# Eight PSUM banks of a pre-norm transformer layer shared out anew: four for scores and three for the ring, in place of three and four

## The reference

```
h   = ln(x);  q, k, v = h @ Wq + bq, h @ Wk + bk, h @ Wv + bv        (per head: 2048 x 16)
s   = q k^T / 4 + slope[head] * (key - 2047);  s = -inf where key > query
y   = x + (softmax(s) v) @ Wo + bo
W'  = clip(round(W / (mean|W| + 1e-8)), -1, 1)    for w1, w2 (704 x 256) and w3 (256 x 704)
g   = ln(y);  out = y + (sigmoid(g W1'^T) * (g W2'^T)) W3'^T
```

## Time and profile before

| | us |
|---|---|
| median of 3 runs | 667.93 |
| the runs | 667.62 to 674.13 |
| the profiled execution's own time | 665.75 |
| its span | 664.0 |

### The profile page before, as it was taken

How to read it: one execution, slowest core, us unless ns; L and a number is a source line. 1 busy time by engine, 2 the same in 40 slices (tenths; PEclk the granted TensorE clock), 3 DMA queues, 4 the chain that set the end, 5 groups by cost and what they waited for, 6 DMA issues and landing times.

```text
span 664.0 us, 11006 instructions
## 1 busy us (share of the span) xinstructions
PE 616.9 (93%) x3710; PEld 378.2 (57%) x3710; DVE 461.9 (70%) x1189; ACT 365.4 (55%) x770; POOL 117.2 (18%) x146
## 2 busy tenths in 40 slices
PE   1888898899999989999999999999999999999997
PEld 1444555556576656455556676555555556665586
DVE  4458878667777876568787778788788888411075
ACT  2424454564464555657656556476676665667521
POOL 5465200031021220420002122003100000123000
PEclk9959898899999999999999999999999999999999
DMA  8664554465121313633231131137141210011000
GB/s 254 173 185 132 147 148 114 114 195 147 34 81 35 97 34 98 182 110 94 54 82 34 34 98 33 49 103 172 39 113 34 68 50 0 2 43 42 1 17 32
DMA packets 27277, 57.65 MB, mean 87 GB/s; under 512 B 5397, under 2 KB 15125, under 8 KB 23637
## 3 DMA queue, kind: packets, MB, share of 16 engines
q1 hardware_dynamic: 27220, 56.95, 31.6%
HBM read 41.87 MB, written 14.80 MB: 85 GB/s over the span
## 4 chain that ended last, share of the span: by engine, by line
PE 76%; DVE 11%; issue 4%; ACT 4%; DMA 3%; SPq 1%; POOL 0%; ACTq 0%; POOLq 0%
PE pS L942 19%; PE pO L955 19%; PE pM L922 17%; PE pM L897 5%; DVE pm L1094 4%; PE pM L843 3%; PE pM L906 3%; DVE pM L1097 3%; PE pS L945 2%; PE pM L883 2%; DMA qst<-mT 2%; ACT probs L787 1%; PE pS L906 1%; PE pS L843 1%; PE pM L849 1%
## 5 line engine op out<-in xcount | busy, mean ns | idle before, releaser
L787 ACT ACTIVATE probs<-pS 128x512 f32<-128x512 f32 (+3 forms) x640 | 304.8, 545 | 191.6 <-PE pS L945 94.8
L1094 DVE TENSOR_REDUCE pm<-pM 128x1 f32<-128x512 f32 x384 | 239.2, 680 | 49.4 <-PE pM L922 49.2
L942 PE MATMUL pS<-qst,kst 128*128 128x512 f32 (+3 forms) x640 | 250.4, 407 | 7.8 <-DMA qst<-mT 4.3
L922 PE MATMUL pM<-kst,qst 126*128 126x512 f32 (+3 forms) x640 | 239.4, 402 | 9.8 <-DVE pm L1097 3.4
L942 PEld LDWEIGHTS pS<-qst,kst 128*128 128x128 f32 x640 | 121.5, 192 | 91.1 <-issue 52.8
L1097 DVE CUSTOM_DVE_ANT_0 pM<-pM,mask 128x128 f32<-128x128 f32 (+3 forms) x256 | 118.5, 518 | 47.3 <-PE pM L922 47.0
L922 PEld LDWEIGHTS pM<-kst,qst 126*128 126x128 f32 x640 | 122.8, 197 | 36.6 <-DVE pm L1097 7.7
L955 PE MATMUL pO<-probs,vals 128*17 128x512 f32 (+3 forms) x1280 | 133.5, 535 | 0.0
L955 PEld LDWEIGHTS pO<-probs,vals 128*17 128x17 f32 x1280 | 29.5, 97 | 64.6 <-issue 41.0
L945 PE MATMUL pS<-maskb,identb 128*128 128x128 bf16 x256 | 58.6, 231 | 0.0
L644 POOL TENSOR_TENSOR rstd<-ve,mhalf 128x4 f32<-128x4 f32 (+1 forms) x9 | 8.5, 946 | 218.9 <-DVE ve L1010 218.8
(11 more groups left out here) (145 smaller groups left out, 426.2 us busy)
## 6 DMA issues: line engine op xcount, KB each, us to landing
kst<-parts SPq DMA_DIRECT2D x80, 256.0 KB
parts<-qk_hl SPq DMA_DIRECT2D x32, 256.0 KB, 3.2
qst<-parts SPq DMA_DIRECT2D x32, 256.0 KB, 4.1
ctx_dram<-ctx_raw SPq DMA_DIRECT2D x15, 256.0 KB, 3.9
xin<-in_L_attn_x SPq DMA_DIRECT2D x5, 512.0 KB, 5.1
out<-work SPq DMA_DIRECT2D x8, 256.0 KB, 2.2
work<-ctx_dram SPq DMA_DIRECT2D x7, 256.0 KB
work<-rden_dram SPq DMA_DIRECT2D x7, 256.0 KB
```

The source lines that it names most:

```text
L787: nc.scalar.activation(probs[:, n % PSLOTS, q0:CH], pS[:, n % SBANKS, q0:CH], ACT.Exp)\
L922: pe.matmul(max_bank(x)[:, 0:N], qst[0:R_MAX, u % QSLOTS, h, t * P:(t + 1) * P], kst[0:R_MAX, n % KSLOTS, h, 0:N], start=True, stop=True). ...
L942: ins = pe.matmul(pS[:, n % SBANKS, q0:CH], kst[0:R_END, sl, h, b:b + P], qst[0:R_END, u % QSLOTS, h, q0:CH], start=True, stop=not is_diag ...
L1094: nc.vector.tensor_reduce(dst, bank, AX.X, ALU.max).then_inc(max_free, 1)
```

## The change

One line: the score banks become four and the ring three. pO keeps its bank. With it change: the bank of every score (n % 4), what it waits for (the exponential four before), the bank of each use of the ring and what it waits for (the use three before), and the places of the head's and the tail's groups (i % 5). In the head the groups numbered 0, 5 and 10 (xT of chunk 0, the second query group of chunk 0, gamma) take the ring, where before 0, 4, 8 and 12 did. The plan of turns and side groups is the same.

```diff
-    SBANKS, RING, SIDE_AFTER = 3, 4, 1
+    SBANKS, RING, SIDE_AFTER = 4, 3, 1
```

## The result

The changed kernel takes 703.09 us (median of 4 runs, 701.78 to 706.54); the kernel before, run beside it on the same chip, takes 671.03 (667.62 to 674.16). The ratio is 1.0487, with a 95% interval of 1.0407 to 1.0567: slower by 4.9%. The forecast was slower, 685.0 with a range of 675 to 698. The direction is right, the size is 18 us short, and the range does not hold it. The profiled executions say the same: 703.06 against 665.75, spans 701.3 against 664.0. So +37.3 us where +17.5 was forecast. By the medians it is +32.1: the profiled execution of the kernel before, 665.75, lies under all four of this set, and 3.1 of the 18 us come from the kernel before itself, 671.03 in this set where the forecast started from 667.93.

A forecast was written before the change was run, and what follows sets the result against it. TensorE's order of issue was taken to bound the kernel; ring 24, score banks -8 and head 1.5 gave +17.5 us on 665.75, 683.3, or 685 with the median 2.2 higher; range 675 to 698.

The forecast's parts named there:

- What bounds the kernel: Plain pairs of steps: TensorE's order of issue sets the time, 5.78 us a pair; VectorE is next, 0.9 us to spare.
- Part 1: Ring of three, nine plain pairs: the last turn before the batch starts 0.29 us late, pair 6.07 us instead of 5.78.
- Part 2: Ring of three, fuller pairs: at most one 0.60 us slot lost per stretch between batches; ring total 24 us, ends 18 and 43.
- Part 3: Four score banks: a fourth bank removes nearly all score waits on exponentials; 8 us gained, ends 4 and 10.
- Under 10 us: Sign at the scores' weight loads: waits of L942 on L787 fall from 26.6 us to under 10.
- Part 4: Head and tail on five places: first score about 2.1 us later, costing 1.5 (ends 0 and 2.1); tail 0.
- A: Rival, faster: score banks bind and VectorE's idle time hides the ring's lateness; only -10 left, 658 us; chance 0.03.
- B: Rival, no change: TensorE headroom absorbs full slots, only plain and half of middle pairs pay; 666 to 668 us; chance 0.07.
- D: Rival, the clock: at 0.95 from 156 to 577 us, 22 us more; with the forecast +40, 707 us; chance 0.02.
- C: Rival, much slower: side groups hold one of three ring banks, every stretch pays a slot; +36, 704 us; chance 0.10.
- the pair of rows 5: Sign: the fuller pair from 547.07 us, whose ninth turn waits for the sixth reduction instead of the fifth, takes 0.6 us more.
- The waits of L922: Sign at the turns' weight loads: their waits on VectorE (L1094 and L1097) grow from 14.5 us to some 35.

The follow-up runs named there:

- e1: Changed kernel with three score banks instead of four, ring of three kept, one bank of PSUM unused: 706.18 us, ratio 1.0596 to the kernel before.
- e2b: Against the kernel before: three score banks, ring of three for turns and swaps only, side groups in their own bank; second run, for its trace: 686.51 us, ratio 1.0282.
- e12: Kernel before with the side group behind the third head instead of the second: 681.53 us, ratio 1.0165.
- e13: Changed kernel with the side group behind the third head instead of the second: 711.37 us, ratio 1.0624 to the kernel before.
- e10: Against the kernel before: three score banks, ring of three for turns only, side groups in their own bank, weighted sums every step: 678.89 us, ratio 1.0143.
- e3: Changed kernel with the head's groups back on four places instead of five: 699.93 us, ratio 1.0509 to the kernel before.
- e11: Changed kernel with the head's and the tail's groups back on their four old places: 700.07 us, ratio 1.0462 to the kernel before.
- e4: Changed kernel with a batch of weighted sums every step instead of every second step: 697.21 us, ratio 1.0457 to the kernel before.
- e5: Kernel before with a batch of weighted sums every step instead of every second step: 668.33 us, ratio 0.9997.
- e9: Kernel before with a batch per step in 33 pairs chosen from e5's timeline, double batches elsewhere: 670.79 us, ratio 1.0036.

## Why the prediction was right or wrong

**What bounds the kernel: right.** TensorE's order of issue sets the time, and one bank fewer makes a user that already waits one slot later: the first up group and the plain pairs show it in the timeline of the changed kernel, and e1 puts the whole loss on the ring.

**Part 1: place and wait right, size 0.12 short.** The last turn of a plain pair is 0.29 us late; the pair takes 6.19 us, not 6.07. The term left out is that a matmul which waits for its bank waits with its weight load, which otherwise runs under the matmul before it. Over nine pairs that is about 1 us.

**Part 2: the step that failed.** It said that the slot is lost "once per stretch between batches and not once per turn, since the waits before it in a stretch are replaced, not added". With no side group in the stretch that holds on the average: the five pairs with over 8 turns lose 0.60 us each in e1, from 0.13 to 0.96. With one, it does not. TensorE makes no turn for 1.06 us and more, and the group holds one of the three banks for 2.10 us, until its reader comes. In the stretch from 241.30 VectorE is dry in front of the group's result and the turn behind it waits for the group's bank; that stretch loses two slots, +1.21 us. Reckoned again by Part 2's own rule from the trace of the kernel before, with the largest lateness of a stretch capped at a slot, some 18 us of its sum fall on the 37 pairs with a side group; they lose 26.5 in e1, more than the 22.2 of one slot each, and 23 of the 37 lose more than a slot. With the group in a bank of its own (e2b) the 37 lose 8.1. So that the sharing costs 16 to 21 us is shown. How it does so is shown for single stretches only: that each dry place of VectorE costs one slot is not, since e12 and e13 speak against it. The cause is not settled to the last microsecond either: e10 leaves 10 us that neither the sharing nor the long batch explains.

A second gap in Part 2: "the rest nothing (few turns, or none)". The seven pairs with 1 to 6 turns lose 4.2 us in e1: 0.5 in each of three pairs with five turns in late units (4.76 to 5.24 us in one), and 1.1 in a pair with six. No run shows why. All pairs together lose 39.0 us to the ring where Part 2 took 24 with an upper end of 43. The upper end was near, with a slot for every stretch; that is a sum that fits, since the single pairs come out anywhere from 2.1 us shorter to 2.9 longer.

**Part 3: at its lower end or in the range, not settled.** Forecast 8 us, ends 4 and 10. The spans of e1 and the changed kernel differ by 3.0, but in these also lie the head's places and a tail that ended 1.5 us later. By the sums of pairs the fourth score bank gives 4.6 us in the changed kernel, 5.4 in e3 and 3.2 in e11. By the medians, each over its own kernel before, it gives 7.4, 6.3 and 8.5; e1 and e3 were timed on one chip in one set, 706.18 against 699.93. The expected gain is there in the pairs without turns, 3.8 us, within the 2 to 4 given for them. In all pairs with turns together the traces of the three kernels have between 1.7 us gained and 0.5 lost. There a score that comes earlier mostly makes the turn behind it wait longer, as the forecast said of the full stretches alone. The estimate also counted waits that are none. The first weight load behind a batch shows 0.85 us of idle time in every kernel here (0.64, 0.42 or 0.21 behind batches that end with a block on the diagonal, whose rows are narrower), and puts it on "issue" or on L787. In the kernel before 18 of the 74 cases on L787 are such, with 7.0 of 27.0 us; in the changed kernel 20 of 31, with 10.0 of 14.3. In e4 with its 159 such places they are the row:

```profile
PEld pS L942 <- ACT probs L787: 101.8, 133, 0.9
```

132 of the 133 stand behind a batch, 101.8 / 133 = 0.77 us each, in a kernel with four score banks. A releaser's name on an idle time of fixed length is not a wait that another bank removes. "Under 10 us" failed for that reason; the waits that are left without it are 4.3 us in 11 cases, from 20.0 in 56.

**Part 4: near in size, one term missing.** The first score starts at 51.84 us, not at 50.73, and the first exponential is 2.0 us later than before. But the head as a whole starts sooner or later from one execution to another: its first turn comes anywhere from 34.1 to 36.1 us. Measured from the first turn to the first exponential it is 16.0 to 16.5 us in the four kernels with the old places and a ring of four (before, e5, e9, e12), 17.0 to 17.3 in the five with the old places and a ring of three (e1, e2b, e10, e3, e11), and 18.0 to 18.4 in the three with the new places (changed, e4, e13). So the new places cost about 1.0 us, where 1.5 was forecast, and the ring's 16 turns 0.9, where nothing was. The sentence that failed is "The head's 16 turns are paced by VectorE with three banks or four". Their masked reductions take 0.3 to 0.73 us, and TensorE's loads wait up to 0.49 us where 0.21 to 0.36 stood before. From the first reduction to the last it is 7.38 us (34.67 to 42.04) where it was 6.52 (34.62 to 41.14). And what the places cost at the first exponential was regained by step 16, as e3 shows. The tail's 0 us is open: it was 1.5 us longer in the changed kernel, e11 and e13, and not in e3 and e4, which have four score banks as well.

**The rivals.** A and B fell with e1: VectorE's idle time and TensorE's supposed headroom hide nothing. D fell with the windows. C, at 704 us, is nearest in time, and its mechanism, side groups that hold one of only three banks, is the largest part. In its own words it is wrong too, and its number was in part luck: not "every stretch pays a slot". Among the 22 pairs of 7 or 8 turns without a side group the mean is 0.24 us, and among those with turns and a side group in both steps 0.82.

**What was to show it.** Of the signs named, these came: the wait before the last turn of a plain pair, the clock, the busy times, the waits of L942 down (14.3 us, not under 10), VectorE's waits for turns up by 21.1 us (24 forecast), the pair of rows 5 longer (6.00 to 6.72 by the exponentials, 0.72 for 0.6). The waits of L922 are 51.6 us for a forecast of 35. "If fuller ones grow by more than 0.6, part 2 is [wrong]" is what happened.

The share of weight loads, which the Trainium skill's page Perfetto Trace Analysis, section Identifying the Most-Contended Engine, takes for TensorE beside the share of the peak rate, would have had room for these waits. Here the weight loads went from 57% to 54% while the time grew by 4.9%; the pitch of the matmuls was the better witness. What the Trainium skill's page TensorE: Matmul & The Clock Gate tells of another kernel in its section "A second HAM failure mode: psum-queue depth-cycling" did not come here: from 169 to 618 us the turns' weight loads waited for VectorE in 123 cases, 39.4 us in all, and the granted clock stayed at 1.00.

## What to carry to other kernels

A ring of n banks gives the reader n - 1 users of cover. Set that, as time (here 0.60 us each), against every stretch in which the producer makes none of them, one by one (here a batch of 1.84 us, a side group of 1.06). Look hardest at other work that takes a bank of the same ring: it is read out later than the common user (2.10 us after its start here), and the users behind it wait for that. Here it was 16 to 21 of some 40 us, and a bank of its own took them away. A cap on the loss of a stretch has to be shown and not assumed. And compare two kernels stretch by stretch: the whole difference between e12 and e13 came out toward a theory that their last 144 steps do not bear out. A wait removed elsewhere gains only where the queue behind it has nothing to wait for.

## What was not expected of the hardware

- A weight load that waits for its bank no longer hides under the matmul before it: the row of its matmul is 0.50 us instead of 0.40, and the next batch starts 0.12 us later.
- Each change from 128-row matmuls to a batch of L955 has 0.32 us from the last turn's start to the batch's first, where turns and scores follow each other every 0.235 us, and the first weight load behind a batch of full width shows 0.85 us of idle time, put on L787 or on "issue". Halving the batches gives 80 more of both, and the kernel before is no slower for it (ratio 0.9997).
